# Changing the order of TensorE's steps in an attention kernel, and adding the causal mask on VectorE

## What is computed

```
x = x + L0(norm(x))   lambda layer: keys softmaxed over positions, content and relative-position parts
x = x + L1(norm(x))   16 heads of 64, softmax(mask(q k^T / 8)) v, then Wo
                      heads 0-7 see keys up to the query (j <= i), heads 8-15 keys from it on (j >= i)
x = x + L2(norm(x))   16 heads of 64 with relative positions in height and width, no mask, bias, then a projection
x = x + relu(L3(norm(x)) + bias)   depthwise 3x3 taps and a channel product given as a tensor train
```

## Time and profile before

| | |
|---|---|
| median of three runs | 1393.41 us |
| profiled execution: its time / its span | 1397.12 us / 1395.3 us |
| TensorE busy | 1337.2 us, 96% of the span, 7792 products |
| VectorE / ScalarE / GpSimd busy | 608.8 (44%) / 436.2 (31%) / 624.7 us (45%) |
| mean granted clock of TensorE | 0.986 of full |

### The profile page before, as it was taken

One profiled execution on the slowest core, in us unless ns is written; L12 is line 12 of the kernel. 1 busy time (PEld: TensorE's weight loads), 2 busy tenths in 40 slices (PEclk: granted clock), 3 DMA queues, 4 the chain that ended last, 5 costly groups with the idle time before them and its releaser, 6 DMA issues.

```text
span 1395.3 us, 20610 instructions
## 1 busy us (share of the span) xinstructions
PE 1337.2 (96%) x7792; PEld 1058.8 (76%) x7792; DVE 608.8 (44%) x1385; ACT 436.2 (31%) x1053; POOL 624.7 (45%) x715
## 2 busy tenths in 40 slices
PE   4899889799999999999999999999999999999998
PEld 3688755457888887788888788788877887877887
DVE  5423422684454324445332455444154654456322
ACT  2230112022434311344330344534114444333222
POOL 2332279025454565545447443443654634445100
PEclk9999989999999999999999999999999999999999
DMA  5111135012222232222223221221322222210012
GB/s 193 38 46 46 31 61 93 0 33 76 69 76 69 68 85 83 76 69 69 69 69 98 69 61 54 62 69 54 91 76 61 61 61 60 63 53 24 1 54 68
DMA packets 57122, 89.23 MB, mean 64 GB/s; under 512 B 6880, under 2 KB 19840, under 8 KB 57024
## 3 DMA queue, kind: packets, MB, share of 16 engines
q1 hardware_dynamic: 55024, 84.59, 22.0%
q10 hardware_dynamic: 2000, 3.32, 0.7%
HBM read 79.50 MB, written 4.19 MB: 60 GB/s over the span
## 4 chain that ended last, share of the span: by engine, by line
PE 81%; DVE 3%; issue 2%; ACT 1%; POOL 0%; ACTq 0%; DVEq 0%; POOLq 0%
PE PS L1018 51%; PE PS L1495 5%; PE PS L1074 4%; PE PS L1092 3%; PE PS L858 3%; PE PS L1106 2%; PE PS L1062 2%; PE PS L864 2%; PE PS L1116 2%; PE PS L1135 2%; PE PS L1512 2%; DVE part L842 1%; PE PS L876 1%; PE PS L1083 1%; PE PS L1067 1%
## 5 line engine op out<-in xcount | busy, mean ns | idle before, releaser
L1018 PE MATMUL PS<-XB,w_hi 128*128 128x512 f32 x1024 | 355.7, 404 | 3.4 <-DVE XB L392 3.4
L212 POOL CAST w_hi<-w_raw 128x512 fp32r<-128x512 f32 x195 | 121.8, 624 | 398.6 <-PE PS L1018 290.8
L214 POOL TENSOR_TENSOR w_lo<-w_raw,w_hi 128x512 fp32r<-128x512 f32 x195 | 254.8, 1307 | 15.6
L1018 PEld LDWEIGHTS PS<-XB,w_hi 128*128 128x128 f32 x1024 | 192.6, 188 | 50.1 <-issue 7.2
L1018 PE MATMUL PS<-XB,w_lo 128*128 128x512 f32 x512 | 200.5, 392 | 0.0
L1018 PE MATMUL PS<-XB,part 128*128 128x512 f32 x768 | 197.1, 401 | 0.0
L1215 ACT ACTIVATE part<-PS,nmax 128x256 f32<-128x256 f32 (+1 forms) x256 | 111.3, 457 | 170.7 <-DVE nmax L1308 107.0
L1018 PEld LDWEIGHTS PS<-XB,part 128*128 128x128 f32 x768 | 140.9, 189 | 28.8
L212 POOL CAST part<-part 128x512 fp32r<-128x512 f32 x85 | 52.3, 615 | 148.1 <-PE PS L1018 147.7
L1018 PE MATMUL PS<-part,w_hi 128*128 128x512 f32 x344 | 113.2, 396 | 1.1 <-DVE part L1361 1.1
L214 POOL TENSOR_TENSOR part<-part,part 128x512 fp32r<-128x512 f32 x85 | 110.4, 1299 | 6.8
(11 more groups left out here) (142 smaller groups left out, 2031.0 us busy)
## 6 DMA issues: line engine op xcount, KB each, us to landing
w_raw<-in_w SPq DMA_DIRECT2D x187, 256.0 KB, 2.6
part<-in_w SPq DMA_DIRECT2D x85, 256.0 KB, 2.6
part<-part SPq DMA_DIRECT2D x32, 128.0 KB, 4.5
out_x<-xT SPq DMA_DIRECT2D x16, 256.0 KB, 2.1
xT<-in_x ACTq DMA_DIRECT2D x8, 256.0 KB, 8.4
xT<-in_x SPq DMA_DIRECT2D x8, 256.0 KB, 11.2
w_raw<-in_w SPq DMA_DIRECT2D x16, 128.0 KB, 3.7
part<-in_emb ACTq DMA_DIRECT2D x1, 961.0 KB, 13.2
```

The source lines that it names most:

```text
L212: pool.tensor_copy(hi, raw).then_inc(w_hi_done, 1)
L214: pool.tensor_tensor(lo, raw, hi.bitcast(F32), ALU.subtract).then_inc(w_ready, 1)
L1018: m = nc.tensor.matmul(PS[:, bank, :], wt[:, (c % 4) * P:(c % 4) * P + P], rhs(hl, c), start=c == k == 0, stop=c == CK - 1 and k == 2)
```

## The change

Six things change, in one edit:

1. **Mask.** The four bf16 products per `scores(i, a)` in layer 1 go. `maxima` adds the mask to both diagonal blocks of a head in one VectorE instruction (256 elements per row, in place in PSUM, mask from SBUF), waits for it, and then takes the two maxima.
2. **Order within an item.** `attend(i-1, 1)` moves behind item i-1's V, directly ahead of `scores(i, 0)`; `attend(i, 0)` now directly precedes `scores(i, 1)`, and `relative(i+1)` follows these; `turn_probs(i, 0)` stands alone after Q; the second half's chunks are cut differently. ScalarE's and VectorE's queues follow.
3. **Start.** Item 0 takes Q, K and V chunk by chunk together for the first four chunks; V goes to bank 4; the weights' order follows.
4. **Ends of stages.** Output blocks use banks 6 and 7, so the next scores no longer wait for the last add; `turn_values` and `attend` of the next item do.
5. **Last item.** Four chunks of the last V, and the first halves of three output blocks, move between its steps; the output blocks rotate over three banks.
6. **L3's matrix.** `build_m` is spread by a table, so that its last product comes before the last half block; the first channel products wait for the adds one by one.

```diff
         def out_bank(s, o):
-            return (0 if s == 3 else S) + o % 2
+            return (1, X, 0)[o % 3] if s == 3 else O + o % 2
+    M_AFTER = {(0, 0): (), (1, 0): (), (2, 0): (), (0, 1): (0, 1), (1, 1): (2, 3), (2, 1): (4, 5), (3, 0): (6,), (3, 1): (7,),
+               (4, 0): (8,), (4, 1): (9,), (5, 0): (10, 11), (5, 1): (12,), (6, 0): (13,), (6, 1): (14,), (7, 0): (15,), (7, 1): ()}
...
-                            nc.tensor.matmul(PS[:, S + hh, at + lo:at + hi], x[rows, qs], y[rows, cols],
-                                             start=qt == k == 0, stop=False, skip_group_check=True)
-                for hh in range(2):
-                    for qt in range(2):
-                        at = qt * N + qt * P
-                        m = nc.tensor.matmul(PS[:, S + hh, at:at + P], identb[:, :], maskb[:, int(ahead_of(i)), :],
-                                             start=False, stop=True, skip_group_check=True)
-                    m.then_inc(s_done, 1)
+                            m = nc.tensor.matmul(PS[:, S + hh, at + lo:at + hi], x[rows, qs], y[rows, cols],
+                                                 start=k == 0, stop=k == 2)
+                            if (qt, k) == (1, 2):
+                                m.then_inc(s_done, 1)
...
+        for c in range(4):
+            for kind in "QKV":
+                project(0, kind, range(c, c + 1))
         for kind in "QKV":
-            project(0, kind, range(CK))
-        for i in range(ITEMS):
-            final = i == ITEMS - 1
+            project(0, kind, range(4, CK))
+        for i in range(ITEMS - 1):
+            stage_ends = i % PAIRS == PAIRS - 1
+            if i % PAIRS:
+                attend(i - 1, 1)
             scores(i, 0)
             project(i + 1, "Q", range(0, 4))
             turn_values(i)
             project(i + 1, "Q", range(4, CK))
+            turn_probs(i, 0)
+            project(i + 1, "K", range(0, 3))
+            attend(i, 0)
             scores(i, 1)
-            turn_probs(i, 0)
-            project(i + 1, "K", range(0, 2))
-            attend(i, 0)
             relative(i + 1)
-            project(i + 1, "K", range(2, 6))
+            project(i + 1, "K", range(3, CK))
+            project(i + 1, "V", range(0, 2))
             turn_probs(i, 1)
-            project(i + 1, "K", range(6, CK))
-            attend(i, 1)
-            project(i + 1, "V", range(CK))
...
+            if stage_ends:
+                project(i + 1, "V", range(2, 4))
+                attend(i, 1)
+                project(i + 1, "V", range(4, CK))
                 for o in range(CK):
+                    out_block(i // PAIRS, o, range(CK))
+            else:
+                project(i + 1, "V", range(2, 4 if i == ITEMS - 2 else CK))
+        i = ITEMS - 1
+        attend(i - 1, 1)
+        scores(i, 0)
+        project(i, "V", range(4, CK))
+        out_block(3, 0, range(0, 3))
+        scores(i, 1)
+        out_block(3, 0, range(3, 4))
+        turn_values(i)
+        turn_probs(i, 0)
+        out_block(3, 1, range(0, 4))
+        attend(i, 0)
+        out_block(3, 2, range(0, 2))
+        turn_probs(i, 1)
+        out_block(3, 2, range(2, 4))
+        attend(i, 1)
@@ attention_act, the order of the queue
             evac_v(i)
+            if i % PAIRS:
+                evac_o(i - 1)
             exps(i, 0)
-            evac_q(i + 1)
+            if i + 1 >= LO_KEYS:
+                evac_q(i + 1)
             evac_t(i, 0)
+            if i + 1 < LO_KEYS:
+                evac_q(i + 1)
             exps(i, 1)
             evac_relative(i + 1)
+            evac_k(i + 1)
             evac_t(i, 1)
@@ attention_dve
+                    on_diagonal = PS[:, S + n % 2, :].rearrange("p (a n) -> p a n", a=4)[:, 0::3, :]
+                    mask = maskb[:, int(ahead_of(i)):int(ahead_of(i)) + 1, :].broadcast_to([P, 2, P])
+                    nc.vector.tensor_tensor(on_diagonal, on_diagonal, mask, ALU.add).then_inc(masked, 1)
+                    dve.wait_ge(masked, n + 1)
...
             maxima(i, 0)
+            if j:
+                rest_of_o(i - 1)
             normalize(i, 0)
```

More of the change, by code:

```diff
@@ L161, in build, with take, take_item @@
         sources = [None] * CK + list(range(CK, HB0))
[L162 to L168, removed]
+        slots = {}
+        def take(key, layer, kind, number, halves=range(2)):
+            for half in halves:
+                slots[key, half] = len(sources)
+                sources.append(block_at[layer, kind, number, half])
+        def take_item(i, halves=range(2)):
             for kind in "QKV":
-                take((i, kind), STAGES[i // PAIRS][0], kind, i % PAIRS)
-        take_item(0)
+                take((i, kind), STAGES[i // PAIRS][0], kind, i % PAIRS, halves)
+        take_item(0, (0,))
+        take_item(0, (1,))
         for i in range(ITEMS):
@@ L175, in build @@
                 take_item(i + 1)
+            if i == ITEMS - 1:
+                for half in range(2):
+                    for o in range(3):
+                        take((3, "O", o), 2, "O", o, (half,))
             if i % PAIRS == PAIRS - 1:
-                for o in range(CK):
+                for o in range(3 if i == ITEMS - 1 else 0, CK):
                     take((i // PAIRS, "O", o), STAGES[i // PAIRS][0], "O", o)
@@ L1032, in project @@
                     pe.wait_ge(k_lo, min(i, LO_KEYS))
-                if c == 0 and kind == "V":
+                if i and c == 0 and kind == "V":
                     pe.wait_ge(q_hi, i + 1)
                     pe.wait_ge(q_lo, i + 1)
-                if i == 0 and c == 0 and kind in "QK":
-                    evacuated(pe, len(groups) - 8 + PJ[kind])
+                if i == c == 0:
+                    evacuated(pe, len(groups) - 8 + bank_of(i, kind))
                 if i % PAIRS == 0 and kind == "Q":
                     norm.ready(i // PAIRS, c)
-                chunk_of(first_slot[i, kind], c, lambda hl, c: x_part(hl, h, c), PJ[kind])
+                chunk_of((i, kind), c, lambda hl, c: x_part(hl, h, c), bank_of(i, kind))
         def scores(i, a):
@@ L1079, in turn_values @@
             pe.wait_ge(v_evac, i + 1)
+            if i % PAIRS == 0 and i:
+                pe.wait_ge(sum_done, CK * (i // PAIRS))
             if i:
@@ L1139, in out_block @@
             for c in chunks:
-                if c == 0 and o >= 2:
-                    pe.wait_ge(sum_done, CK * s + o - 1)
-                if c == 0 and o == 0 and s < 3 or o < 2 and c == CK - 1:
+                beside = 3 if s == 3 else 2
+                if c == 0 and o >= beside:
+                    pe.wait_ge(sum_done, CK * s + o - beside + 1)
+                if c == 0 and o == 0 and s < 3:
                     pe.wait_ge(o_hi, PAIRS * (s + 1))
                     pe.wait_ge(o_lo, PAIRS * (s + 1))
[L1145 to L1149, removed]
+                if s == 3 and o == 0:
+                    pe.wait_ge(o_hi, PAIRS * s + c + 1)
+                    pe.wait_ge(o_lo, PAIRS * s + c + 1)
+                if c == 0 and o == 1 and s in (1, 2):
+                    pe.wait_ge(relh_evac, PAIRS * (s - 1) + 1)
+                    pe.wait_ge(relw_evac, PAIRS * (s - 1) + 1)
+                if c == 0 and o == 1 and s == 3:
+                    pe.wait_ge(v_ready, ITEMS)
+                chunk_of((s, "O", o), c, lambda hl, c: (oh, ol)[hl][:, c, :], out_bank(s, o))
         def build_m(i):
@@ new lines, in attention_pe @@
+        i = ITEMS - 1
[13 more added lines that the diff above has]
+        attend(i, 1)
+        for o in range(CK):
+            for half in range(0 if o >= 3 else 1, 2):
+                out_block(3, o, range(4 * half, 4 * half + 4))
+                for k in M_AFTER[o, half]:
+                    build_m(k)
@@ L1392, in attention_dve @@
                 rest_of_k(i + 1)
-            rest_of_o(i)
+            if j == PAIRS - 1:
+                rest_of_o(i)
             if j == 0:
@@ L1402, in attention_dve @@
                 for o in range(CK):
-                    if s == 3:
-                        rest_of_m(dve, 2 * o)
+                    for k in M_AFTER[o, 0] if s == 3 else ():
+                        rest_of_m(dve, k)
                     add_out(s, o)
@@ L1407, in attention_dve @@
                         stats_of(s, o - 1)
-                    if s == 3:
-                        rest_of_m(dve, 2 * o + 1)
+                    for k in M_AFTER[o, 1] if s == 3 else ():
+                        rest_of_m(dve, k)
                 stats_of(s, CK - 1)
@@ L1488, in channel_product @@
                         pe.wait_ge(u_lo, 4 * (b - 1) + bank + 1)
-                    elif bank < 2:
-                        pe.wait_ge(sum_done, 4 * CK)
+                    elif bank < 3:
+                        pe.wait_ge(sum_done, 4 * CK - 2 + bank)
                     for c in range(CK):
```

57 lines of the change are left out of this document (22 added, 35 removed).

## The result

The changed kernel takes 1374.49 us (median of four runs, 1374.09 to 1375.83) against 1394.41 for the kernel before beside it: ratio 0.9860, 95% interval 0.9843 to 0.9877. The profiled execution took 1374.09 us, its span 1372.3. Lines of the new file: 1033 is 1018 of before (weight products), 1075 is 1062 and 1083 is 1074 (scores), 1129 is 1116 and 1119 is 1106 (attention), 1103 is 1092 and 1094 is 1083 (transposes), 1147 and 1148 are 1134 and 1135 (relative terms), 1175 is 1157 and 1542 is 1495 (L3's matrix and first product), 1246 is 1215, 1360 is 1318, 1344 is the new mask add.

A forecast was written before the change was run, and what follows sets the result against it. TensorE, 96% busy, was taken to bound the kernel, so work taken from it counts in full. Terms 6.1 + 4.5 - 4.8 + 4.6 + 3.0 + 4.8 + 1.1 = 19.3 us gave 1374.1 us by the median; range 1366 to 1382.

The forecast's parts named there:

- 1. mask products: Layer 1's score halves: removing the mask products saves 0.19 us in each of 32 halves, 6.1 us.
- 2. layer 1, 30 direct passages: Layer 1 items: attention directly beside scores saves 0.15 us at each of 30 places, 4.5 us; ends 0 and 9.3.
- 2. layer 2, scores before the relative terms: Layer 2 items: scores between attention and relative terms cost 0.30 us, 16 times, 4.8 us lost.
- 3. start: Item 0's projections: interleaved Q, K, V chunks fill TensorE's waits, gain 4.6 us, despite a new wait for Q's second half.
- 4. stage ends: Stage ends: three waits for the last add go, 3.3 us, less 0.3 for possibly late turn_probs(8, 0); gain 3.0 us.
- 5. last item: Last item: waits and half clock get products in front of them, gain 4.8 us; 1.7 if the clock falls as long.
- 6. before L3: Before L3: the wait for M's last remainder goes, but 2 us remain before the second channel products; gain 1.1 us.
- The add: VectorE's new mask add in layer 1, two per score half: 0.43 us each, hidden behind TensorE's work.
- The way in: Layer 1: entering attention's column tiles from the whole array costs 0.1 us, beside 0.21 for the way out.
- The new wait before `scores(31, 1)`: Last item: ScalarE's exponentials end late after the last V, so TensorE waits 1.3 us.
- Cover: Layer 1: turn_probs(i, 0) has 6.2 us for VectorE's maxima, remainder of O and normalizing, which need some 4.8.
- The slower rival: Mask adds run as slowly as VectorE's worst; slower than before from 1.42 us per add; chance 4%, partial loss 5%.

The follow-up runs named there:

- e2: Changed kernel with the mask put back as four identity products per score half, new order kept; 1380.04 us.
- e1: Kernel before, in its own order, with only the mask moved to one VectorE add per head; 1387.26 us, ratio 0.9948 to before.
- e4: Changed kernel with one chunk of K moved between attend(i, 0) and scores(i, 1) in layer 1, splitting one direct passage per item; 1379.15 us.
- e3: Changed kernel with the relative-position products directly behind attend(i, 0) and scores(i, 1) behind them; 1373.47 us.
- e5: Changed kernel with each mask add made three times; 1406.18 us, ratio 1.0085 to the kernel before.
- e7: Changed kernel with edits against four remaining waits: item 0's chunk order, last item's exponentials before V, build_m's table, earlier channel-bank reads; 1368.63 us.

## Why the prediction was right, step by step

| step | predicted | measured | from |
|---|---|---|---|
| 1. mask products | 6.1 | 6.0 to 6.2 | e2, e1 |
| 2. layer 1, 30 direct passages | 4.5 | 5.6 to 6.0 | whole items, two passages each: 22.41 in e1 to 22.04, 22.80 before to 22.40 in e2 |
| 2. layer 2, scores before the relative terms | -4.8 | -3.7 to -4.0 | 16 x 0.25, item against item of before; the first items of its two stages lost 0.05 and 0.08 |
| 3. start | 4.6 | 4.1 | stretch |
| 4. stage ends | 3.0 | 3.3 | 1.10, 1.20 and 1.02: those three items, less their masks and passages |
| 5. last item | 4.8 | 3.2 | to the end of the output blocks (61.9 to 61.5, with 2.75 of V more in it) |
| 6. before L3 | 1.1 | 1.0 | 25.5 to 24.5 after the last block |
| sum | 19.3 | 19.4 to 19.9 (19.7 by the span) | |

That the sum came within a microsecond is in part luck. Step 2 was too low by 1.1 to 1.5 us in layer 1 and by 0.8 to 1.1 in layer 2; step 5 was too high by 1.6 and step 3 by 0.5. The errors cancel.

- **The bound** was read rightly: with TensorE busy throughout and at pace, products taken away counted in full, and 27 us of VectorE's adds cost nothing.
- **The add** took 0.427 us, predicted 0.43. The Trainium skill's rule (page "SBUF — State Buffer", section "Who interferes with whom") is that an instruction with at most one SBUF input, outside the modes that take both of VectorE's port pairs, does not contend with GpSimd. For the adds it held: by the start and end times of each in this trace, 31 of them met no GpSimd work and took 427 ns on average, 15 lay beside its cast (423) and 16 beside its subtraction (431). The prediction left out the condition on those modes, and the multiplications, with one SBUF input too, did not go free (last section). It also gave a support that the trace of before doesn't: the 0.68 us of the earlier trace rows, at 442.09, was not beside GpSimd's splitting, which had ended at 442.04.
- **Step 2 in layer 1 was mis-sized.** I put the passage from column to row tiles at half of what the two ways over the array cost. It costs less: between weight products 0.21 to 0.22 are saved (e4), of 0.31 at most. In whole items it is 0.19 to 0.20, and the rows of e1 give a reason for the lower end: one of the ways out that lie between e1 and the changed kernel, from scores to transposes, costs 0.15 and not 0.21. The Trainium skill's rule that a change of mode drains TensorE (page "TensorEngine Tiling (Array Packing)", section "Key Properties") agrees in sign in both layers; for the size there are only the rows. The way in, 0.1 of the 0.31, rested on a stream of 0.64 us for attention that no row shows; the runs bear out ways out and in together, not that part by itself.
- **Step 2 in layer 2** was right in its mechanism, and e3 shows that by itself. Its 0.32 per item is more than the 0.25 that the change cost, because e3's order is also 0.07 us per item better than before's.
- **Step 3:** the wait for Q's second half was 1.23 us, with 0.95 predicted; the slack of VectorE's remainders held. The 4.1 depends on one execution of before, too: e1, with the same code there, took 23.94 us and not 22.47, since half clock was granted for 6.8 us and not for 3.4.
- **Step 4:** the 0.3 us that I charged for VectorE's statistics did not appear; e5 is the only kernel in which that item (25.53) is longer than its neighbours.
- **Step 5** rested on one execution. The waits and the half clock in the earlier trace rows include a fall of the clock that the same code doesn't always meet: e1 leaves that stretch untouched, and from the first scores of item 31 to the first channel product it took 62.2 us at full clock, where the kernel before took 64.7. Windows of before and of e1:

```profile
1215.10:1279.80 64.70, 59.83 (x278) 47.90 (x277) 36.79 (x57) 24.78 (x38) 30.13 (x30) 0.95 0.18 49
```
```profile
1207.20:1269.40 62.20, 56.89 (x277) 45.91 (x275) 36.94 (x57) 24.92 (x38) 30.23 (x30) 1.00 0.18 51
```

  So of the 3.2 us measured some 2.4 are the clock of that execution, and against e1 the gain is 0.8. The fall stands in one of the two profiles with the old order and in none of the eight with the new one; that the new order prevents it is not shown. The new wait before `scores(31, 1)` came as predicted (1.05 and the restart, ScalarE's exponentials being the last to end), and one that I had not seen came beside it: `build_m` twice in a row at three places running, 0.5 and 0.2 us for the remainder of M. e7 took both away.
- **Cover:** what I had wrong without paying for it is the slack before `turn_probs(i, 0)`. I put it at 1.4 us. In the trace VectorE ends its normalizing at 406.3 and the transposes start at 406.6, so 0.3 us were left, because the pair of multiplications at 403.67 takes 1.96 us beside GpSimd's splitting.
- **The slower rival** needs adds of over 1.42 us each. e5 made them 1.29 in sum (three of 0.43), and was already slower than before by 11.5 us: the point lies lower than I gave it, since I counted one wait per item where there are two. At 0.427 the kernel stays well away from it.

Open: how many of before's median microseconds the clock's falls make. Between executions they move by some 3 us in layer 0 alone, so that differences of medians (4.2 in e2, 2.4 in e3) and of stretches (6.0, 3.5) don't match closer than that.

## What to carry to other kernels

Where TensorE has no waits, count the changes of its tiling as work: here each direct passage in place of a way over the whole array was worth about 0.2 us, scores put between attention and the relative terms cost 0.25 to 0.32, and the same neighbours helped in one layer and hurt in the other. Put groups of the same tiling side by side, and judge an order by its effect on a single repeated item, which repeats to a hundredth of a microsecond, not by the medians. When work moves to an engine with slack, compute the slack of each reader behind it: here an add of 0.43 us per head was free, and three of them cost 31 us.

## What the hardware showed beyond that

- Multiplications in SBUF on VectorE are slowed by GpSimd's splitting; the adds that read PSUM aren't. The group of 128x128 multiplications went from 287 ns on average to 602 without any change of its own, since the new order puts it beside the splitting. Taken one by one in the trace after, they took 283 ns where GpSimd was idle (26 of them) and 957 where its subtraction covered more than half of them (23); for 128x256 it was 351 and 936. The mask adds beside it took 431.

```profile
L1360 DVE TENSOR_SCALAR part<-part,prec 128x256 f32<-128x256 f32 x192 | 86.0, 476 | 3.4
L1360 DVE TENSOR_SCALAR part<-part,prec 128x128 f32<-128x128 f32 x64 | 38.5, 602 | 1.1
```

- The direct passage from products on 64-column tiles to products on 64-row tiles costs about 0.1 us. That is an estimate: the ways out and in that it replaces were put at 0.31, and 0.21 of it is saved (e4).
- Half clock was granted for different lengths in the same code: 3.4 or 6.8 us near 42 us, 10.2 or 13.7 near 172 us. Behind the waits of the last item it came in the profile of before and not in that of e1.
